# Four token tiles per weight block in the first two matmuls of a mixture-of-experts FFN, with eight PSUM banks instead of four

## The reference

```python
x = x + 0.5 * ffn(layernorm(x), ...)
x = x + attn(layernorm(x), ...)     # causal top-8 neighbours, softmax, message, gelu
x = x + 0.5 * ffn(layernorm(x), ...)

def ffn(xf, gate_w, w1, w2, w3):    # 8 experts, DIM 1024, D_FF 2048, top 2
    probs = softmax(einsum('td,ed->te', xf, gate_w))
    weights, idx = top_k(probs, 2); weights /= sum(weights)
    x1 = silu(einsum('td,efd->tef', xf, w1))
    x3 = einsum('td,efd->tef', xf, w3)
    out_all = einsum('tef,edf->ted', x1 * x3, w2)
    return sum over the two chosen experts of out_all * weights
```

## Time and profile before

| | |
|---|---|
| runs shown | 2: 6547.99 and 7419.93 us |
| median of these | 6983.96 us |
| profiled execution | 6550.55 us, its span 6549.0 us (core 5, the slowest; the fastest 6540.7) |
| TensorE granted clock, mean over the span | 0.936 to 0.937 of 2.4 GHz, all cores alike |
| instructions in the profile | 71344 |

### The profile page before, as it was taken

How to read it: one execution, slowest core, us unless ns; L and a number is a source line. 1 busy time by engine, 2 the same in 40 slices (tenths; PEclk the granted TensorE clock), 3 DMA queues, 4 the chain that set the end, 5 groups by cost and what they waited for, 6 DMA issues and landing times.

```text
span 6549.0 us, 71344 instructions; the slowest of 8 cores (6540.7 to 6549.0 us)
## 1 busy us (share of the span) xinstructions
PE 5903.9 (90%) x26310; PEld 2605.8 (40%) x26310; DVE 2390.8 (37%) x4354; ACT 807.3 (12%) x1360; POOL 345.9 (5%) x666
## 2 busy tenths in 40 slices
PE   4699999999999999995445579999999999999998
PEld 1244444444444444441112134444444444444443
DVE  3333333333333333334554433333333333333333
ACT  1111111111111111111111211111111111111110
POOL 0000000000000000000000000000000000000000
PEclk7799999999999999996666779999999999999999
DMA  2122222222222222220000012222222222222223
GB/s 59 21 38 36 39 36 39 38 38 39 38 37 39 36 39 39 38 38 0 0 0 0 0 26 39 35 37 36 39 36 39 38 38 39 39 36 39 38 38 81
DMA packets 93507, 222.86 MB, mean 34 GB/s; under 512 B 10612, under 2 KB 10868, under 8 KB 92788
## 3 DMA queue, kind: packets, MB, share of 16 engines
q0 software_dynamic: 92592, 201.52, 20.4%
q1 hardware_dynamic: 580, 16.79, 0.8%
HBM read 411.34 MB, written 8.39 MB: 64 GB/s over the span
## 4 chain that ended last, share of the span: by engine, by line
PE 89%; DVE 6%; ACT 2%; issue 2%; DVEq 0%; DMA 0%; ACTq 0%; SPq 0%
PE ps L220 88%; DVE xn L382 1%; PE ps L226 1%; DVE arena L377 1%; ACT arena L320 1%; DVE top L706 1%; DMA lmls<-lm 0%; DVE negmax L744 0%; ACT arena L748 0%; DVE arena L727 0%; DVE arena L776 0%; DVE arena L714 0%; DVE arena L658 0%; DVEq L727 0%; DVE arena L762 0%
## 5 line engine op out<-in xcount | busy, mean ns | idle before, releaser
L220 PE MATMUL ps<-xn,w1p 128*128 128x512 bf16 x8192 | 1952.9, 382 | 0.9
L220 PE MATMUL ps<-xn,w3p 128*128 128x512 bf16 x8192 | 1943.6, 380 | 0.0
L220 PE MATMUL ps<-arena,w2p 128*128 128x512 bf16 x8192 | 1773.3, 379 | 0.0
L565 DVE TENSOR_TENSOR x3b<-ps,arena 128x512 bf16<-128x512 f32 x1024 | 708.1, 691 | 2328.8 <-PE ps L220 2328.8
L220 PEld LDWEIGHTS ps<-xn,w1p 128*128 128x128 bf16 x8192 | 803.6, 98 | 988.8 <-issue 32.6
L220 PEld LDWEIGHTS ps<-xn,w3p 128*128 128x128 bf16 x8192 | 804.7, 98 | 977.0 <-issue 18.5
L220 PEld LDWEIGHTS ps<-arena,w2p 128*128 128x128 bf16 x8192 | 801.6, 98 | 966.5
L561 ACT ACTIVATE s1b<-ps 128x512 bf16<-128x512 f32 x1024 | 611.5, 597 | 4660.3 <-PE ps L220 4660.3
L609 DVE TENSOR_TENSOR x_fm<-x_fm,ps 128x512 f32<-128x512 f32 x1024 | 704.1, 688 | 1046.9 <-PE ps L220 1046.9
L571 DVE TENSOR_TENSOR arena<-s1b,x3b 128x512 bf16<-128x512 bf16 x1024 | 435.9, 426 | 109.2 <-DVE x3b L565 3.7
L532 POOL DMA_DIRECT2D w1p<-w x256 | 136.5, 533 | 4221.4 <-PE ps L220 4151.4
(11 more groups left out here) (103 smaller groups left out, 1067.2 us busy)
## 6 DMA issues: line engine op xcount, KB each, us to landing
w1p<-w POOLq DMA_DIRECT2D x256, 256.0 KB, 4.3
w3p<-w POOLq DMA_DIRECT2D x256, 256.0 KB, 5.0
w2p<-w POOLq DMA_DIRECT2D x128, 512.0 KB, 8.0
y<-x_fm SPq DMA_DIRECT2D x2, 4096.0 KB, 18.5
wqt<-wq POOLq DMA_DIRECT2D x1, 64.0 KB, 30.2
wkt<-wk POOLq DMA_DIRECT2D x1, 64.0 KB, 30.2
x_fm<-x SPq DMA_DIRECT2D x1, 30.5
gbt<-gb SPq DMA_DIRECT2D x1, 8.0 KB, 30.7
```

The lines of the kernel that those rows point to most:

```text
L220: t.matmul(out, lhsT, rhs, start=start, stop=stop),
L565: lambda v, x3sl=x3sl, b3=b3, j=j: v.tensor_tensor(x3sl, ps[b3][:, :], self.c_rep[:, j * TW:(j + 1) * TW], ALU.mult),
```

## The change

In a k-iteration of the FFN the loops over tiles and chunks are exchanged. First all 32 matmuls of w1 run, chunk by chunk, the four tiles one after the other with the same weight block, into banks 0 to 3; then the 32 of w3 into banks 4 to 7. Only the last chunk's matmul of each tile raises the semaphore, in both kernels. After them come the silu and the two multiplications of each tile, with the tile's own token (`x1_stop[j]`, `x3_stop[j]`). `s1b` and `x3b` have four buffers instead of two and move into the arena, and `h_half` moves 2 KB up there. The w2 loop, the coefficients and all other phases are as they were.

```diff
-        self.s1_free = [None, None]
-        self.x3_free = [None, None]
+        self.s1_free = [None] * NJ
+        self.x3_free = [None] * NJ
@@
-        self.s1b = E(nc.sbuf_tensor("s1b", [128, 2 * TW], BF16)).ap()
-        self.x3b = E(nc.sbuf_tensor("x3b", [128, 2 * TW], BF16)).ap()
@@
-        self.h_half = vbf(32768, NK * T)
+        self.s1b = vbf(25600, 4 * TW)
+        self.x3b = vbf(29696, 4 * TW)
+        self.h_half = vbf(34816, NK * T)
@@
-                    for j in range(NJ):
-                        b1 = j % 2
-                        b3 = 2 + j % 2
-                        sslot = j % 2
-                        for c in range(NCH):
+                    x1_stop = [None] * NJ
+                    x3_stop = [None] * NJ
+                    lastmm1 = lastmm3 = None
+                    for c in range(NCH):
+                        for j in range(NJ):
                             lastmm1 = self.mm(
-                                ps[b1][:, :], w1sl[:, c * 128:(c + 1) * 128],
+                                ps[j][:, :], w1sl[:, c * 128:(c + 1) * 128],
                                 self.xn[:, c * T + j * TW: c * T + (j + 1) * TW],
                                 start=(c == 0), stop=(c == NCH - 1),
-                                waits=[xn_tok, tok_w1, self.bank_free[b1]],
+                                waits=[xn_tok, tok_w1, self.bank_free[j]],
                                 inc="PE" if c == NCH - 1 else None)
-                        for c in range(NCH):
+                            if c == NCH - 1:
+                                x1_stop[j] = lastmm1
+                    for c in range(NCH):
+                        for j in range(NJ):
                             lastmm3 = self.mm(
-                                ps[b3][:, :], w3sl[:, c * 128:(c + 1) * 128],
+                                ps[4 + j][:, :], w3sl[:, c * 128:(c + 1) * 128],
                                 self.xn[:, c * T + j * TW: c * T + (j + 1) * TW],
                                 start=(c == 0), stop=(c == NCH - 1),
-                                waits=[xn_tok, tok_w3, self.bank_free[b3]],
+                                waits=[xn_tok, tok_w3, self.bank_free[4 + j]],
                                 inc="PE" if c == NCH - 1 else None)
-                        s1sl = self.s1b[:, sslot * TW:(sslot + 1) * TW]
-                        x3sl = self.x3b[:, sslot * TW:(sslot + 1) * TW]
+                            if c == NCH - 1:
+                                x3_stop[j] = lastmm3
+                    for j in range(NJ):
+                        s1sl = self.s1b[:, j * TW:(j + 1) * TW]
+                        x3sl = self.x3b[:, j * TW:(j + 1) * TW]
                         ts1 = p.emit("scalar", ... AF.Silu ...
-                                     waits=[lastmm1, self.s1_free[sslot]], inc="SC")
+                                     waits=[x1_stop[j], self.s1_free[j]], inc="SC")
                         tx3 = p.emit("vector", ... ps times c_rep ...
-                                     waits=[lastmm3, crep_ready, self.x3_free[sslot]],
+                                     waits=[x3_stop[j], crep_ready, self.x3_free[j]],
                                      inc="VE")
                         th = p.emit("vector", ... s1sl times x3sl into h_half ...
                                     waits=[ts1, tx3, self.h_free], inc="VE")
-                        self.bank_free[b1] = ts1
-                        self.bank_free[b3] = tx3
-                        self.s1_free[sslot] = th
-                        self.x3_free[sslot] = th
+                        self.bank_free[j] = ts1
+                        self.bank_free[4 + j] = tx3
+                        self.s1_free[j] = th
+                        self.x3_free[j] = th
                         h_tile_last[j] = th
                     self.w1_free[slot] = lastmm1
                     self.w3_free[slot] = lastmm3
```

More of the change, by code:

```diff
@@ L524, in ffn @@
                 h_tile_last = [None] * NJ
-                lastmm1 = lastmm3 = None
                 for k in range(NK):
@@ L560, in ffn @@
+                    for j in range(NJ):
+                        s1sl = self.s1b[:, j * TW:(j + 1) * TW]
+                        x3sl = self.x3b[:, j * TW:(j + 1) * TW]
                         ts1 = p.emit("scalar",
-                                     lambda s, s1sl=s1sl, b1=b1: s.activation(
-                                         s1sl, ps[b1][:, :], AF.Silu),
-                                     waits=[lastmm1, self.s1_free[sslot]], inc="SC")
+                                     lambda s, s1sl=s1sl, j=j: s.activation(
+                                         s1sl, ps[j][:, :], AF.Silu),
+                                     waits=[x1_stop[j], self.s1_free[j]], inc="SC")
@@ L564, in ffn @@
                         tx3 = p.emit("vector",
-                                     lambda v, x3sl=x3sl, b3=b3, j=j: v.tensor_tensor(
-                                         x3sl, ps[b3][:, :],
+                                     lambda v, x3sl=x3sl, j=j: v.tensor_tensor(
+                                         x3sl, ps[4 + j][:, :],
                                          self.c_rep[:, j * TW:(j + 1) * TW], ALU.mult),
-                                     waits=[lastmm3, crep_ready, self.x3_free[sslot]],
+                                     waits=[x3_stop[j], crep_ready, self.x3_free[j]],
```

## The result

| | before | changed |
|---|---|---|
| executions | 42 | 43 |
| lowest | 6547.8 us | 6602.1 us |
| median | 6938.2 us | 6632.9 us |
| ratio, without the executions named below | | 1.0067, 95% interval 1.0043 to 1.0091 |

What follows compares the result with a forecast made beforehand. The prediction took TensorE's stream of matmuls to bound the kernel (busy 5903.9 of 6549.0 us). 6550.6 + 32 (turns) + 10 (seams) gave 6593 us, 0.6% more; the sum's own range was 6570 to 6620, the whole 6560 to 6655.

Steps and rivals of the forecast that it cites:

- Stream, loads, banks, transfers at nothing: FFN k-loop: 16,384 weight loads as before, matmuls at unchanged pitch, bank rotation and transfers free; each taken as 0.
- the 28 us of the lower end: w1 and w3 matmuls: most gained if three of four loads go and the pitch's excess over column streaming with them.
- The rotation's 16 us: w1 and w3 matmuls, each in another bank than the one before: upper end, 0.001 us more on 16,384; taken as 0.
- The steady iteration: k-iteration: VectorE's run of four pairs, 1.41 us each, frees bank 7 with 3.0 us slack; cost 0.
- The turn, 32 us: From k-loop into w2: first w2 matmul waits for tile 0's last product, 1.0 us idle, 32 times.
- The seam's wait, 10 us: Ahead of each expert: second w1 matmul waits for the fourth coefficient copy, 0.6 us, 16 times; bounds 7 and 10.
- The falls at the seams, taken at 0 with +22 as the upper end: TensorE clock falls at fourteen seams between experts: +22 us if all fell twice, -25 if none; taken as 0.
- The word "same": Whole kernel: result within about 2%, what a measurement can tell from no change; chance 0.91.
- Rival A: Turn into w2: the pause lowers the clock, 54 us more, 6647 us, or 6702 with double falls; chance 0.12.
- Rival B: k-iterations: bank rotation makes TensorE pause and the clock keep falling, 433 us if once per iteration, 7026 us; chance 0.04.
- Rival C: w1 and w3 matmuls: weight reuse pays as loads are left out, 6565 us or even 5389; chance 0.06.
- Rival D: k-iteration: VectorE's run of eight holds a bank too long, each us beyond 3.0 more costs 256 us; chance 0.01.

Runs made afterwards that it cites:

- 1: Changed kernel with the weight loads of three of four w1 and w3 matmuls left out; cores 6597.0 to 6599.2 us, ratio to before 1.0089.
- 2: Changed kernel with the last of the eight k-iterations in the tile order of before; 6552.6 to 6555.8 us, ratio to before 0.9993.
- 5: Changed kernel with only the last w2 matmul of each group waiting for k = 7, and w2 in eight banks; 6551.4 to 6553.6 us on cores 4 to 7.
- 6: Changed kernel with w2 starting at tile 1 instead of tile 0; 6617.4 to 6632.3 us.
- 3: Kernel before with each expert's first w1 matmul also waiting for the fourth coefficient copy; 6552.2 to 6555.0 us on cores 0 to 3.
- Experiment 4: Changed kernel with the four coefficient matmuls in banks 0 to 3 instead of 0, 1, 0, 1; 6580.1 to 6583.2 us, ratio to before 1.0037.
- 8: Kernel before with the next expert's four coefficient matmuls moved, in a row, into the w2 loop; 6528.0 to 6533.6 us.
- experiment 10: Kernel before with coefficient matmuls in the w2 loop, one ahead of each tile's groups; 6523.1 to 6529.6 us on cores of its two quickest timed executions.

## Why the prediction was right or wrong

- **Stream, loads, banks, transfers at nothing:** right. Loads 26,310 as before; pitch 0.216 us. Leaving the loads out (1) shows that the 28 us of the lower end were not to be had either. The rotation's 16 us did not come: 13.81 us for 64 matmuls.
- **The steady iteration:** right, slack was even larger. L570 follows L576 within 0.34 to 0.47 us of its start where I took 0.61, so a pair is 1.14 to 1.26 us, not 1.41.
- **The turn, 32 us:** right in place, cause and size. 1.00 us, with the handoff of 0.15 us from the earlier trace rows, 32 times; taken away by two different means (2, 5) and doubled (6).
- **The seam's wait, 10 us:** right in place and nearly in size; the pause itself is 0.58 us at the half clock; over the fourteen seams that is 8 us, and about 8 by experiment 2.
- **The falls at the seams, taken at 0 with +22 as the upper end:** this is the step that failed. It was +16 on core 4 (+20 if the overlap with the wait is charged to the falls). I saw that the falls were of three kinds and treated them as a mean that stays. They are not drawn at random: cores 4 and 5 of before show the same fourteen kinds in the same order. Each seam loses about 0, 1.7 or 3.3 us, and which it is hangs on more than what the seam holds: pauses that added 2.6 us to the interval turned a mixture into fourteen double ones, and taking 2.0 of them away again (2, 5) made fourteen single ones of the same seams. That the longer wait itself did it, my first explanation after the result, is refuted by 2 and 3.
- **The sum:** 42 us forecast, 56 measured from the first seam, 53 on the span of core 4; 6593 forecast against about 6603, where the executions without a stretch of 0.81 lie (6602.1 to 6604.3). The ratio, 1.0067, lies on the forecast 1.0065, but by luck: it averages over executions of both kernels with such stretches of 0.81 on a pair of cores. Between the lowest executions, 6547.8 to 6552.0 us before (seven) and these twelve of the change, it is 0.8%. The median of 6632.9 holds such a stretch on a pair of cores, which my range, though it covers the number, had no term for.
- **The word "same":** the most likely class was "within 2%", and 0.67% is within it. But the interval excludes 1, so the measurement told apart more than the 2% that I put down as its limit: the change is a small loss, not no change.
- **Rival A** (clock falls at the turn): refuted for the change, no fall at any of 256 turns with 1.0 us of pause. At 2.1 us (6) the clock fell at 14 of 256, so the mechanism exists, but not at this pause. **Rival B**: refuted; the clock inside an expert reads 1.00. The Trainium skill's warning (TensorE: Matmul & The Clock Gate, "A second HAM failure mode: psum-queue depth-cycling") is not borne out by rotation over eight banks: no idle time between groups, 13.81 us for 64 matmuls, and no fall of the clock inside an expert. **Rival C**: refuted by 1. **Rival D**: no such wait.

What stays open: what sets the instants at which the clock falls, and with it why thirteen or all fourteen seams of the change fell twice. Experiments 2, 5 and 6 leave the seam as it is in the change and alter only the turns, the nearest 55 us ahead of it: the fourteen seams fall once each in 2 and 5, and ten once and four twice in 6 (core 0). Experiment 4 has both kinds in turn, and 8 all three, each with one and the same code. So what a seam holds doesn't settle it, and when it comes is what is left; that the interval between experts decides is argued from this, not shown.

## What to carry to other kernels

Before keeping a weight block for several tiles, compare the pitch of the matmuls with their columns over the clock: where the two agree, the load is hidden and there is nothing to gain. Exchanging tile and chunk loops makes all tiles end at once, so look at whoever waits for the first tile after the loop, and put that wait on the one matmul that needs it. Short stretches of matmuls over few rows between full ones are worth breaking up or moving, and their cost in clock has to be read place by place, since pauses of 2.6 us in an interval of 337 moved it by 16 us here.

## What was unexpected of the hardware

- TensorE's clock falls to its 1.2 GHz level, for 1.7 or 3.3 us of lost time, after 3.5 us of fp32 matmuls over 8 rows although the engine is busy without a gap (14.00 of 14 us, clock 0.76 or 0.88), at 8 of 14 places on core 6 of experiment 8. Pairs of them, 1.8 us with full matmuls around, never did it at 14 places on 8 cores. fp32 matmuls over all 128 rows held 1.00 for 22 us, and those over one row stayed at 0.50 for 11 us without a gap. A pause of 1.0 us amid full matmuls lowered the clock at none of 256 turns, one of 2.1 us at 14 of 256.
- Going from bf16 matmuls over 128 rows to fp32 ones over 8 and back costs 0.29 us; whether the type or the rows cost it is not separated.
- A pair of neighbouring cores ran at 0.81 for some 160 us of one execution, 30 us of its span, while the other six read 1.00. The Trainium skill (TensorE: Matmul & The Clock Gate, part 1) tells of a current limit at 13/16 of the clock, 0.8125, which would fit the value; it says that the whole die goes there once three of its cores run dense matmuls, and stays while the load lasts. Here it was two cores of a die, for a fortieth of the span, with the same matmuls before and behind it. In the profiled execution of experiment 10 (7503 us) it was all eight cores, for some 5,300 to 5,600 us each, and each pair of neighbours went there and came back by itself.
